# A kernel of recurrence, routing and six attention layers: the attention mask written by ACT instead of added by PE

## The chip, the cores and the metric

The kernel runs on one core of one Trainium2 chip. The core has a matrix engine (PE, whose weight loads are shown apart as PEld), three engines for elementwise work (DVE, ACT, POOL), a queue engine (SP) that issues transfers, and a PSUM memory of eight banks of 128 partitions by 512 float32 columns, into which PE writes. The metric is the device time of one execution in microseconds (us); lower is better.

## The reference

The reference has four parts, one after the other, on 16 sequences of 256 tokens with 128 channels: a gated recurrence, a routed feed-forward, a small linear attention, and a stack of six layers that takes most of the time. Each of the six layers is a local attention with 16 heads of 64 channels and a feed-forward. What the change touches is the attention:

```python
q, k = l2norm(q) * qs, l2norm(k) * ksc      # and a rotary turn
bq = q.reshape(b, h, nw, w, d)              # windows of w = 32 tokens
bk2, bv2 = look(bk), look(bv)               # own window and the one before: 64 keys
mask = (it < jb) | (it > jb + w) | (jb == -1)
sim = jnp.einsum('bhwie,bhwje->bhwij', bq, bk2) * QK_SCALE
sim = jnp.where(mask, -jnp.finfo(sim.dtype).max, sim)
attn = jax.nn.softmax(sim, -1)
out = jnp.einsum('bhwij,bhwje->bhwie', attn, bv2)
```

## The kernel before, in words

After a prologue for the first three parts, the six layers run as one software pipeline. A unit u is one layer with one of eight windows (NC = 8), 48 units in all (NU); a step n handles a quarter of a unit, four of the 16 sequences, so there are 192 steps (NG). Each engine has its own loop over n, written out by hand in its order, and semaphores join them. In its step n each engine works on several stages of different quarters at once; below, "step 0" to "step 3" are the steps with n % 4 (called q4) of 0 to 3, and four of them are a round.

On PE a step holds: the projections `proj(n, 0..5)` (line 550; parts 0 and 1 are q, 2 and 3 are k, 4 and 5 are v), transposed probabilities, products with the values, the output projection, and once a round the pieces of the feed-forward. For the quarter n - 2 it holds the key transposes `turn_k(n - 2, 0)` and `turn_k(n - 2, 1)` (line 570), the mask, and the scores `sim(n - 2)` (line 595): 128 small products into banks 4 and 5, one bank for each parity of the heads. Then come the query transposes of quarter n (line 560).

The scores of a bank are 128 rows (4 sequences by 32 queries) by 8 heads by 64 keys. `mask` (line 582) opens each bank: a product of a 32-row identity, idb, with a 512-column mask, mkb, both bf16, puts 0 or -1e36 into every column, with the flag that starts a sum. The score products then add to it. The two mask products use different rows of the array. idb and mkb are made once, at the start, by five ACT instructions (lines 1266 and 1270) from kc, a tile of constants that holds the mask for the 64 keys of one head, in three forms (first window, and two orders of the key buffer).

On ACT a step holds evacuations of banks: squares of q and k (`square`, 1358), values (`v_out`, 1366, tile vst), turned keys (`turned_k`, 1384, into kT, which the trace calls big), turned queries (`turned_q`, 1373), probabilities (1397), outputs (`out_turned`, 1405), the exponential (`exps`, 1390), and once a round gelu (1476), a shifted copy, and the copies of the norm (1448, 1449). DVE reads the scores (`largest`, 1049, and `lessened`, 1060, which raises v_sm and after which banks 4 and 5 are free) and turns q and k (1027, 1029); POOL scales and adds (1692, 1678, 1684, 1700).

Banks 2 and 3 are handed from use to use in program order: `claim` makes PE wait for whoever empties the bank. The second key transposes are in bank 2 and are emptied by `turned_k(n - 2, 1)`; the next user of bank 2 on PE is `variance` (651) in step 3, the third part of `gate` (674) in step 1, and the query transposes in the others. `sim` itself waits for both copies of the keys (a_tk). The last projection, part 5, uses bank 3. Lines in the profile are those of this kernel:

Of the kernel before, what the change touches and what calls it, by code (L numbers as in the profile page):

```python
# [8 lines left out]
BF16 = mybir.dt.bfloat16  # L9
# [147 lines left out]
def program(nc, x_d, kc_d, wa_d, wb_d, ba_d, tab_d, qs_d, wqkv_d, wo_d, w1_d, w2_d, vec_d, we_d, out_d, keep_d, xsort_d, ysort_d):  # L157
    with ExitStack() as ctx:
        def sb(name, shape, dt=F32):
# [21 lines left out]
        mkb = sb("mkb", [2 * W, 3, 512], BF16)  # L181
        idb = sb("idb", [2 * W, P], BF16)
# [34 lines left out]
            a_sq a_vst a_tq a_tk a_exp a_p2 a_oev a_xf a_hi a_halo a_mb a_x2s a_halo2 a_ln a_xn a_xh a_w1 a_gelu a_e a_w  # L217
# [160 lines left out]
        def _(eng):  # L378
# [195 lines left out]
            def mask(g):  # L574
                if not 0 <= g < NG:
                    return
                c = g // 4 % NC
                pe.wait_ge("a_mb", 5)
                for par in range(2):
                    pe.wait_ge("v_sm", 2 * (g - 1) + par + 1)  # L580
                    rows = slice(W * par, W * par + W)
                    eng.matmul(bank[4 + par][:, :], idb[rows, :], mkb[rows, 0 if c == 0 else 1 + c % 2, :], start=True, stop=False)  # L582

            def sim(g):
# [5 lines left out]
                pe.wait_ge("g_zero", 1)  # L590
                for r in range(8):
                    for par in range(2):
                        rows = slice(64 * par, 64 * par + 64)
                        for b in range(4):
                            m = eng.matmul(bank[4 + par][32 * b:32 * b + 32, 64 * r:64 * r + 64], qT[rows, g % 2, r, 32 * b:32 * b + 32],  # L595
                                           kT[rows, r, :, 4 * i + b, :], start=False, stop=(r == 7))
# [134 lines left out]
            for n in range(NG + 2):  # L731
# [28 lines left out]
                mask(n - 2)  # L760
# [479 lines left out]
        def _(eng):  # L1240
# [23 lines left out]
            msk = kc[0:2 * W, KC["mask"]].rearrange("p (v k) -> p v k", v=3)  # L1264
            for v in range(3):
                eng.activation(mkb[:, v, :].rearrange("p (r k) -> p r k", r=8), msk[:, v, :].unsqueeze(1).to_broadcast([2 * W, 8, 64]), ACT.Copy,
                               scale=1.0, bias=0.0).then_inc(s["a_mb"], 1)
            for n in range(2):
                rows = slice(W * n, W * n + W)
                eng.activation(idb[rows, :].rearrange("p (b t) -> p b t", b=4), kc[rows, rows].unsqueeze(1).to_broadcast([W, 4, W]), ACT.Copy,  # L1270
                               scale=1.0, bias=0.0).then_inc(s["a_mb"], 1)
# [565 lines left out]
```

## Time and profile before

| | us |
|---|---|
| median of 3 runs | 3678.64 |
| lowest and highest run | 3673.33, 3685.43 |
| span of the profiled execution (first to last instruction) | 3676.2 |
| PE busy in it | 3451.3 (94%) |
| DVE, ACT, POOL busy | 2806.8 (76%), 2365.2 (64%), 2815.1 (77%) |
| mean granted PE clock | 0.973 |

The profile gives no time of the profiled execution beyond its span; the span is 2.4 us below the median of the runs. Busy time is the union of an engine's instructions, and since matmuls are pipelined and their ends modelled, a PE that is busy all the time can still have gaps of issue inside. The timeline gives start and length of each instruction, with equal neighbours merged (x3); the chain of waits is followed back from the last instruction, at each step to what released it.

### The profile page before, as it was taken

The numbers are of one execution on the slowest core, as the hardware profiler recorded it, in microseconds if no ns is written. First come the engines' busy times: TensorE is split into PE (matmuls) and PEld (weight loads), VectorE is DVE, ScalarE is ACT, GpSimd is POOL, SyncE is SP. The second block draws the span as 40 slices with busy tenths as digits, with TensorE's granted clock in tenths as the row PEclk, the third lists the DMA queues.
The fourth block names the chain that finished last, engine by engine and source line by source line (L and its number), as shares of the span: only waits on it lengthen the run. The fifth ranks groups of instructions, "written<-read, shape, count | busy, mean of one in ns | idle before, by whom it ended". The sixth has DMA issues, their size and how long they took to land.

```text
span 3676.2 us, 148973 instructions
## 1 busy us (share of the span) xinstructions
PE 3451.3 (94%) x64612; PEld 2721.5 (74%) x64612; DVE 2806.8 (76%) x4876; ACT 2365.2 (64%) x4307; POOL 2815.1 (77%) x3470
## 2 busy tenths in 40 slices
PE   3799986999999999999999999999999999999997
PEld 2566544788877888777888778877788887788775
DVE  3477666888887888878888878887788888788863
ACT  3333223677766777777777677776677777777663
POOL 1355546998887888878888888888788888888772
PEclk9799997999999999999999999999999999999999
DMA  3333212111111111211111121112111111112110
GB/s 100 98 97 93 87 31 58 47 43 39 46 47 49 40 41 44 51 44 42 45 38 46 44 52 39 42 43 52 40 46 42 40 45 50 44 40 50 36 43 24
DMA packets 126733, 183.48 MB, mean 50 GB/s; under 512 B 29824, under 2 KB 61440, under 8 KB 126080
## 3 DMA queue, kind: packets, MB, share of 16 engines
q1 hardware_dynamic: 119232, 146.15, 15.8%
q0 software_dynamic: 6848, 27.80, 2.5%
q8 instruction: 511, 8.37, 1.0%
q14 instruction: 142, 1.16, 0.1%
HBM read 59.01 MB, written 14.16 MB: 20 GB/s over the span
## 4 chain that ended last, share of the span: by engine, by line
PE 85%; POOL 5%; DVE 3%; issue 3%; ACT 1%; DMA 1%; SPq 0%; ACTq 0%; POOLq 0%; DVEq 0%
PE bank L550 22%; PE bank L622 10%; PE bank L633 9%; PE bank L595 7%; PE bank L560 5%; PE bank L570 4%; PE bank L606 4%; PE bank L696 3%; PE bank L674 3%; PE bank L685 3%; PE bank L582 2%; PE bank L465 1%; PE bank L525 1%; PE bank L642 1%; PE bank L504 1%
## 5 line engine op out<-in xcount | busy, mean ns | idle before, releaser
L550 PE MATMUL bank<-wqkv,xs 128*128 128x512 f32 x3456 | 1061.5, 423 | 17.1 <-DVE m L1029 13.1
L1684 POOL TENSOR_TENSOR m<-m 128x512 f32<-128x512 f32 x576 | 728.7, 1285 | 45.2 <-DVE m L1029 42.6
L550 PEld LDWEIGHTS bank<-wqkv,xs 128*128 128x128 f32 x3456 | 582.8, 191 | 146.0 <-issue 56.9
L1029 DVE TENSOR_TENSOR m<-bank,tab 128x512 f32<-128x512 f32 x768 | 521.5, 679 | 0.7 <-POOL m L1684 0.3
L1358 ACT ACTIVATE sq<-bank 128x512 f32<-128x512 f32 x768 | 458.5, 597 | 98.1 <-PE bank L550 54.2
L1692 POOL TENSOR_TENSOR S<-S,nw 128x1024 f32<-128x1024 f32 x192 | 383.3, 1996 | 168.0 <-DVE S L1060 168.0
L1040 DVE TENSOR_REDUCE ss<-sq 128x8 f32<-128x512 f32 x768 | 504.9, 674 | 0.0
L1700 POOL TENSOR_TENSOR S<-S,rs 128x512 f32<-128x512 f32 x384 | 411.0, 1091 | 69.7 <-DVE rs L1074 67.9
L622 PEld LDWEIGHTS bank<-P,big 64*64 64x64 f32 x24576 | 379.6, 135 | 79.8 <-issue 72.3
L1027 DVE TENSOR_TENSOR m<-bank,tab 128x512 f32<-128x512 f32 x576 | 392.1, 681 | 57.4 <-ACT sq L1358 41.9
L633 PE MATMUL bank<-OT,wo 128*128 128x128 f32 x3072 | 389.9, 282 | 40.8 <-ACT P L1397 27.6
L622 PE MATMUL bank<-P,big 64*64 64x32 f32 x24576 | 401.9, 220 | 4.2 <-issue 3.2
L633 PEld LDWEIGHTS bank<-OT,wo 128*128 128x128 f32 x3072 | 371.8, 198 | 44.9 <-issue 44.6
L1366 ACT ACTIVATE vst<-bank 128x512 f32<-128x512 f32 x384 | 229.6, 598 | 272.6 <-PE bank L550 258.3
L1373 ACT ACTIVATE qT<-bank 128x512 f32<-128x512 f32 x384 | 210.1, 596 | 245.7 <-PE bank L560 245.4
L1684 POOL TENSOR_TENSOR mk<-mk,m 128x512 f32<-128x512 f32 x192 | 242.4, 1285 | 101.0 <-DVE m L1029 101.0
L595 PEld LDWEIGHTS bank<-big,qT 64*32 64x32 f32 x24576 | 265.0, 105 | 64.8 <-issue 62.8
L1049 DVE TENSOR_REDUCE mx<-bank 128x8 f32<-128x512 f32 x384 | 246.9, 684 | 84.5 <-PE bank L595 83.2
L595 PE MATMUL bank<-big,qT 64*32 64x64 f32 x24576 | 299.1, 226 | 6.5 <-issue 5.9
L1027 DVE TENSOR_TENSOR mk<-bank,tab 128x512 f32<-128x512 f32 x192 | 131.5, 685 | 197.7 <-ACT sq L1358 197.6
L1067 DVE TENSOR_REDUCE mx<-S 128x16 f32<-128x1024 f32 x192 | 232.4, 1210 | 16.9 <-ACT S L1390 14.2
L1060 DVE TENSOR_TENSOR S<-bank,mx 128x512 f32<-128x512 f32 x384 | 245.1, 679 | 0.0
(232 smaller groups left out, 6457.1 us busy)
## 6 DMA issues: line engine op xcount, KB each, us to landing
big<-vst SPq DMA_DIRECT2D x1536, 64.0 KB
stage<-in_wqkv SPq DMA_DIRECT2D x36, 256.0 KB, 3.0
tab<-in_tab SPq DMA_DIRECT2D x48, 128.0 KB, 2.2
xsort<-big SPq DMA_DIRECT2D x4, 960.0 KB, 8.6
big<-xsort SPq DMA_DIRECT2D x12, 256.0 KB, 4.5
ysort<-big SPq DMA_DIRECT2D x12, 256.0 KB, 3.6
wo<-in_wo SPq DMA_DIRECT2D x6, 512.0 KB, 3.7
big<-in_x SPq DMA_DIRECT2D x8, 256.0 KB, 3.4
```

Source lines behind the costliest of these rows:

```text
L550: m = eng.matmul(pb[:, :], xt[a], wqkv[:, z, 512 * part:512 * part + 512], start=(n == 0), stop=(n == 2))
L595: m = eng.matmul(bank[4 + par][32 * b:32 * b + 32, 64 * r:64 * r + 64], qT[rows, g % 2, r, 32 * b:32 * b + 32], kT[rows, r, :, 4 * i + b, ...
L622: m = eng.matmul(bank[6 + par][half:half + 64, 128 * k + 32 * b:128 * k + 32 * b + 32], V2[rows, 4 * i + b, 64 * r:64 * r + 64], P2[rows, ...
L633: m = eng.matmul(pb[:, 0:128], wo[:, r, :], OT[:, g % 2, r, :], start=(r == 0), stop=(r == 7))
L1027: eng.tensor_tensor(turned(g, part).rearrange("p (h d) -> p h d", d=DH), pv, ct.unsqueeze(1).to_broadcast([P, 8, DH]), ALU.mult)
L1029: eng.tensor_tensor(m2[:, s3, :].rearrange("p (h s d) -> p h s d", s=2, d=DH // 2), pw, sn.rearrange("p (s d) -> p s d", s=2).unsqueeze(1) ...
L1040: eng.tensor_reduce(ss[:, g // 2 % 2, a:a + 8], sq[:, part % 2, :].rearrange("p (h d) -> p h d", d=DH), axis=X_AX, op=ALU.add).then_inc(s[ ...
L1049: eng.tensor_reduce(mx[:, g % 2, 0, :].rearrange("p (r q) -> p q r", q=2)[:, par], bank[4 + par][:, :].rearrange("p (r k) -> p r k", r=8), ...
L1358: eng.activation(sq[:, part % 2, :], bank[part % 2][:, :], ACT.Square, scale=1.0, bias=0.0).then_inc(s["a_sq"], 1)
L1684: eng.tensor_tensor(turned(g, part), turned(g, part), m2[:, part % 2, :], ALU.add).then_inc(s["g_add"], 1)
L1692: eng.tensor_tensor(S16, S16, nw[:, g // 2 % 2, 1, 32 * (g % 2):32 * (g % 2) + 16].unsqueeze(2).to_broadcast([P, 16, 64]), ALU.mult).then_ ...
L1700: eng.tensor_tensor(S8, S8, rs[:, g % 2, 8 * h:8 * h + 8].unsqueeze(2).to_broadcast([P, 8, 64]), ALU.mult).then_inc(s["g_pn"], 1)
```

## The change

`mask` goes from PE. ACT gets `masked(g)`: for each of banks 4 and 5 one copy from kc, the 64 mask columns repeated for the eight heads, into the whole bank. It stands in ACT's step between the exponential (and what follows it in some steps) and `v_out(n, 0)`. It waits for v_sm as the product did, and for two prologue users of the banks. The scores wait for it by a new semaphore, a_mk; no product starts the sum in banks 4 and 5 any more, all of them add. The tiles mkb and idb and the five instructions that made them are gone.

```diff
--- before.py
+++ after.py
@@ -178,8 +178,6 @@
         zero = sb("zero", [P, NB])
         xs = sb("xs", [P, 2, 2, N], F32R)
         xf = sb("xf", [P, N])
-        mkb = sb("mkb", [2 * W, 3, 512], BF16)
-        idb = sb("idb", [2 * W, P], BF16)
         sq = sb("sq", [P, 2, 512])
         m1 = sb("m1", [P, 4, 512])
         m2 = sb("m2", [P, 2, 512])
@@ -214,7 +212,7 @@
             v_half v_rec v_u v_x1 v_x2 v_x3 v_rt v_xt v_rk v_he v_sh v_rb v_fs v_fn v_pr v_tq v_rc
             g_z g_n1 g_n2 g_n3
             p_proj p_tq p_tk p_sim p_pt p_av p_wo p_lnc p_lnv p_lnb p_fg p_fa p_fw p_ec p_ev p_eb
-            a_sq a_vst a_tq a_tk a_exp a_p2 a_oev a_xf a_hi a_halo a_mb a_x2s a_halo2 a_ln a_xn a_xh a_w1 a_gelu a_e a_w
+            a_sq a_vst a_tq a_tk a_exp a_p2 a_oev a_xf a_hi a_halo a_mk a_x2s a_halo2 a_ln a_xn a_xh a_w1 a_gelu a_e a_w
             v_w1 v_xl v_k v_ss v_sm v_max v_sum v_rec2 v_res v_lo v_ln v_xn v_h v_X v_back v_e v_out v_w
             g_zero g_add g_scl g_sub g_pn g_ch g_tab""".split()
         sems = {n: ctx.enter_context(nc.semaphore(n)) for n in names}
@@ -571,16 +569,6 @@
                 m.then_inc(s["p_tk"], 1)
                 vacant[RING["tk"][h]] = [("a_tk", 2 * g + h + 1)]
 
-            def mask(g):
-                if not 0 <= g < NG:
-                    return
-                c = g // 4 % NC
-                pe.wait_ge("a_mb", 5)
-                for par in range(2):
-                    pe.wait_ge("v_sm", 2 * (g - 1) + par + 1)
-                    rows = slice(W * par, W * par + W)
-                    eng.matmul(bank[4 + par][:, :], idb[rows, :], mkb[rows, 0 if c == 0 else 1 + c % 2, :], start=True, stop=False)
-
             def sim(g):
                 if not 0 <= g < NG:
                     return
@@ -588,12 +576,13 @@
                 pe.wait_ge("a_tq", 2 * g + 2)
                 pe.wait_ge("a_tk", 2 * g + 2)
                 pe.wait_ge("g_zero", 1)
+                pe.wait_ge("a_mk", 2 * g + 2)
                 for r in range(8):
                     for par in range(2):
                         rows = slice(64 * par, 64 * par + 64)
                         for b in range(4):
                             m = eng.matmul(bank[4 + par][32 * b:32 * b + 32, 64 * r:64 * r + 64], qT[rows, g % 2, r, 32 * b:32 * b + 32],
-                                           kT[rows, r, :, 4 * i + b, :], start=False, stop=(r == 7))
+                                           kT[rows, r, :, 4 * i + b, :], start=False, stop=(r == 7), skip_group_check=True)
                 m.then_inc(s["p_sim"], 1)
 
             def probs(g, h):
@@ -757,7 +746,6 @@
                 turn_k(n - 2, 0)
                 proj(n, 3)
                 turn_k(n - 2, 1)
-                mask(n - 2)
                 proj(n, 5)
                 if q4 == 3:
                     variance(u - 2)
@@ -1261,14 +1249,6 @@
                         eng.activation(h[:, :, t], step_in[:, n % 2, :], ACT.Tanh, scale=1.0, bias=0.0).then_inc(s["a_rec"], 1)
 
             ac.wait_ge("d_kc", 32)
-            msk = kc[0:2 * W, KC["mask"]].rearrange("p (v k) -> p v k", v=3)
-            for v in range(3):
-                eng.activation(mkb[:, v, :].rearrange("p (r k) -> p r k", r=8), msk[:, v, :].unsqueeze(1).to_broadcast([2 * W, 8, 64]), ACT.Copy,
-                               scale=1.0, bias=0.0).then_inc(s["a_mb"], 1)
-            for n in range(2):
-                rows = slice(W * n, W * n + W)
-                eng.activation(idb[rows, :].rearrange("p (b t) -> p b t", b=4), kc[rows, rows].unsqueeze(1).to_broadcast([W, 4, W]), ACT.Copy,
-                               scale=1.0, bias=0.0).then_inc(s["a_mb"], 1)
             for what, c, j in chunk_order("ACT"):
                 if what == "step":
                     steps(c, j, j + 1)
@@ -1383,6 +1363,19 @@
                 d = kT[:, 4 * h:4 * h + 4, c % 2, 4 * i:4 * i + 4, :].rearrange("p r b t -> p r (b t)")
                 eng.activation(d, bank[RING["tk"][h]][:, :].rearrange("p (r t) -> p r t", r=4), ACT.Copy, scale=1.0, bias=0.0).then_inc(s["a_tk"], 1)
 
+            def masked(g):
+
+                if not 0 <= g < NG:
+                    return
+                c = g // 4 % NC
+                v = KC["mask"].start + 64 * (0 if c == 0 else 1 + c % 2)
+                ac.wait_ge("v_rb", NC)
+                ac.wait_ge("v_tq", NC)
+                for par in range(2):
+                    ac.wait_ge("v_sm", 2 * (g - 1) + par + 1)
+                    eng.activation(bank[4 + par][:, :].rearrange("p (r k) -> p r k", r=8), kc[:, v:v + 64].unsqueeze(1).to_broadcast([P, 8, 64]),
+                                   ACT.Copy, scale=1.0, bias=0.0).then_inc(s["a_mk"], 1)
+
             def exps(g):
                 if not 0 <= g < NG:
                     return
@@ -1518,6 +1511,7 @@
                 if q4 == 3:
                     centred(u - 2)
                     end_centred(u - 5)
+                masked(n - 2)
                 v_out(n, 0)
                 square(n, 2)
                 turned_k(n - 2, 0)
```

Three places show how instructions move. First PE in a step 3, around the mask; L570 (L568 after) are the second key transposes, L550 (L548) the last projection, L651 (L640) the variance, L595 (L584) the scores. Before:

```order
L550 MATMUL bank<-wqkv,xs 128x512 [waits v_k]
L550 MATMUL bank<-wqkv,xs 128x512 x2
L570 MATMUL bank<-kc,mk 128x128 [waits a_vst,g_scl]
L570 MATMUL bank<-kc,mk 128x128 x3
L582 MATMUL bank<-mkb,idb 128x512 [waits v_sm] x2
L550 MATMUL bank<-wqkv,xs 128x512 [waits a_tk]
L550 MATMUL bank<-wqkv,xs 128x512 x2
L651 MATMUL bank<-kc,lnx 128x1 [waits a_tk]
L651 MATMUL bank<-kc,lnx 128x1 x3
L595 MATMUL bank<-big,qT 32x64 x64
```

After:

```order
L548 MATMUL bank<-wqkv,xs 128x512 [waits v_k]
L548 MATMUL bank<-wqkv,xs 128x512 x2
L568 MATMUL bank<-kc,mk 128x128 [waits a_vst,g_scl]
L568 MATMUL bank<-kc,mk 128x128 x3
L548 MATMUL bank<-wqkv,xs 128x512 [waits a_tk]
L548 MATMUL bank<-wqkv,xs 128x512 x2
L640 MATMUL bank<-kc,lnx 128x1 [waits a_tk]
L640 MATMUL bank<-kc,lnx 128x1 x3
L584 MATMUL bank<-big,qT 32x64 [waits a_mk]
L584 MATMUL bank<-big,qT 32x64 x63
```

The mask row is gone, so the projection follows the transposes, and the first score product waits for a_mk. Then ACT in a step 3, from the exponential to the first key copy. Before:

```order
L1390 ACTIVATE S<-S 128x1024 [waits g_sub]
L1465 ACTIVATE xnr<-xn 128x512 [waits p_fa,a_xn]
L1448 ACTIVATE lnx<-bank 128x512 [waits p_lnv,p_lnc]
L1449 ACTIVATE lnx<-bank 128x512
L1366 ACTIVATE vst<-bank 128x512 [waits d_v2,p_proj]
L1358 ACTIVATE sq<-bank 128x512 [waits v_ss,p_proj]
L1384 ACTIVATE big<-bank 128x4x128 [waits p_tk]
L1358 ACTIVATE sq<-bank 128x512 [waits v_ss,p_proj]
```

After:

```order
L1383 ACTIVATE S<-S 128x1024 [waits g_sub]
L1458 ACTIVATE xnr<-xn 128x512 [waits p_fa,a_xn]
L1441 ACTIVATE lnx<-bank 128x512 [waits p_lnv,p_lnc]
L1442 ACTIVATE lnx<-bank 128x512
L1376 ACTIVATE bank<-kc 128x512 [waits v_sm] x2
L1346 ACTIVATE vst<-bank 128x512 [waits d_v2,p_proj]
L1338 ACTIVATE sq<-bank 128x512 [waits v_ss,p_proj]
L1364 ACTIVATE big<-bank 128x4x128 [waits p_tk]
L1338 ACTIVATE sq<-bank 128x512 [waits v_ss,p_proj]
```

The two writes into banks stand ahead of the value evacuation (vst). Last, ACT at the start of the program, from its first table load. Before:

```order
L1266 ACT_TABLE_LOAD
L1266 ACTIVATE mkb<-kc 64x512 [waits d_kc]
L1266 ACTIVATE mkb<-kc 64x512 x2
L1270 ACTIVATE idb<-kc 32x128 x2
L1278 ACTIVATE big<-bank,ba 128x512 [waits p_px]
L1282 ACTIVATE big<-bank,hb 128x512 [waits v_half,p_px]
```

After:

```order
L1258 ACT_TABLE_LOAD [waits p_px]
L1258 ACTIVATE big<-bank,ba 128x512 [waits d_kc]
L1262 ACTIVATE big<-bank,hb 128x512 [waits v_half,p_px]
L1246 ACTIVATE big<-big 128x16 [waits a_px]
L1249 ACTIVATE big<-step_in 128x16 [waits v_rec] x22
```

The five instructions on mkb and idb are gone, and the table load comes after the wait for the first product. The orders of DVE, POOL and SP are the same in both.

## Rows read from the trace of the kernel before

**Rows 1.** The page, part 4: chain of waits, share of the span by engine.
```profile
PE 85%; POOL 5%; DVE 3%; issue 3%; ACT 1%; DMA 1%; SPq 0%; ACTq 0%; POOLq 0%; DVEq 0%
```

**Rows 2.** Windows, one round of four steps: length, busy us (instructions) per engine, clock, DMA.
```profile
1803.55:1864.33 60.78, 60.78 (x1303) 49.91 (x1302) 50.04 (x85) 45.05 (x79) 52.36 (x62) 1.00 0.18 43
```

**Rows 3.** Groups by line and shape, PE: busy us, mean ns | idle before.
```profile
L582 PE MATMUL bank<-mkb,idb 32*128 32x512 bf16 x384 | 74.7, 386 | 0.0
```

**Rows 4.** Timeline, step 3 at 1801 us: start us, length us, engine, line, operation.
```profile
1801.39 0.60 ACT L1366 ACTIVATE vst<-bank 128x512 f32<-128x512 f32 x1 [1.81 <-PE bank L550]
...
1801.88 0.60 PE L570 MATMUL bank<-kc,mk 128*128 128x128 f32 x4
...
1802.24 0.94 PE L550 MATMUL bank<-wqkv,xs 128*128 128x512 f32 x3
...
1803.02 0.60 PE L570 MATMUL bank<-kc,mk 128*128 128x128 f32 x4
...
1803.55 0.39 PE L582 MATMUL bank<-mkb,idb 32*128 32x512 bf16 x2
1803.71 0.59 ACT L1384 ACTIVATE big<-bank 128x512 f32<-128x512 f32 x1
...
1803.87 0.97 PE L550 MATMUL bank<-wqkv,xs 128*128 128x512 f32 x3
...
1804.44 1.09 PEld L651 LDWEIGHTS bank<-kc,lnx 128*128 128x128 f32 x8
...
1805.55 1.46 PEld L595 LDWEIGHTS bank<-big,qT 64*32 64x32 f32 x128
```

**Rows 5.** Timeline, the program's last step with score products.
```profile
3590.30 1.08 ACT L1384 ACTIVATE big<-bank 128x512 f32<-128x512 f32 x2 [0.81 <-PE bank L570]
...
3591.44 0.46 PEld L674 LDWEIGHTS bank<-xnr,w1r 128*85 128x85 f32 x3 [0.71 <-ACT big L1384]
...
3592.30 0.93 PE L595 MATMUL bank<-big,qT 64*32 64x64 f32 x71
```

**Rows 6.** Chain of waits, the same place.
```profile
3590.80 0.60 ACT big L1384
...
3591.44 0.93 PE bank L674 x3
```

**Rows 7.** Timeline, step 0 at 1813 us.
```profile
1813.35 1.06 ACT L1390 ACTIVATE S<-S 128x1024 f32<-128x1024 f32 x1
...
1815.39 0.60 ACT L1366 ACTIVATE vst<-bank 128x512 f32<-128x512 f32 x1 [0.98 <-PE bank L550]
...
1816.09 0.60 ACT L1358 ACTIVATE sq<-bank 128x512 f32<-128x512 f32 x1
...
1817.72 0.59 ACT L1384 ACTIVATE big<-bank 128x512 f32<-128x512 f32 x1
...
1818.77 1.49 PE L595 MATMUL bank<-big,qT 64*32 64x64 f32 x128
```

**Rows 8.** Timeline, step 1 at 1829 us.
```profile
1829.68 0.60 ACT L1366 ACTIVATE vst<-bank 128x512 f32<-128x512 f32 x1 [1.00 <-PE bank L550]
...
1832.01 0.59 ACT L1384 ACTIVATE big<-bank 128x512 f32<-128x512 f32 x1
...
1832.97 0.85 PE L674 MATMUL bank<-xnr,w1r 128*85 128x512 f32 x3
...
1833.75 1.58 PE L595 MATMUL bank<-big,qT 64*32 64x64 f32 x128
```

**Rows 9.** Tile mkb: duration ns min/median/max, first and last start us.
```profile
L1266 ACT ACTIVATE mkb<-kc x3: 617/619/635, 6.8 to 7.9; 64x512 bf16<-64x512 f32 x3
```

**Rows 10.** Timeline, step 2 at 1844 us.
```profile
1844.73 0.60 ACT L1366 ACTIVATE vst<-bank 128x512 f32<-128x512 f32 x1 [1.53 <-PE bank L550]
```

**Rows 11.** Timeline, ACT at the program's start.
```profile
9.06 0.69 ACT L1278 ACTIVATE big<-bank,ba 128x512 f32<-128x512 f32 x1
```

**Rows 12.** Chain of waits at a layer's end.
```profile
2050.93 6.75 DMA stage<-in_wqkv x2
```

## The prediction

> **What bounds the kernel now.** I read the chain of waits first: its head puts 85% of the span on PE [rows 1]. Then the busy time of one round of four steps in the steady part: in 60.78 us PE is busy for 60.78, DVE 50, ACT 45, POOL 52, at a granted clock of 1.00, which is the 2.4 GHz level [rows 2]. So every stretch that PE is spared shortens the run, until another engine's result comes too late. The groups by line give the mask products 74.7 us of busy time, 386 ns each where one stood alone, and 192 pairs [rows 3]. That is time of the pair's own; what PE really gives up is read in the timeline, from the start of the work before it to the start of the work after.
>
> **What PE is spared.** In the step at 1801 us the key transposes start at 1803.02 and the next projection at 1803.87, 0.85 us later, with the mask pair between. The earlier key transposes of the same step, with no mask behind them, start at 1801.88 and their projection at 1802.24: 0.36 us [rows 4]. The difference, **0.49 us a step**, is the price of a mask pair on PE with the idle array before and behind it; in 192 steps 94 us.
>
> The Trainium skill (TensorE: Matmul & The Clock Gate, "Back-to-back issue gap") has a matmul of 512 columns cost about 216 ns at the full clock; by that rule the pair, which runs side by side, would be worth 0.22 us a step and 42 us in all. The trace disagrees: the gaps around the pair are its own, since the same handover without it takes 0.36 us.
>
> **What takes the place of the mask.** PE needs ACT's copy of the second key transposes (L1384) soon after: the score products read kT, and where a gate or a variance product comes before them it claims bank 2, which that copy frees. The copy hangs on the square of the projection before it and on the transposes, both older than the mask, so it does not move when the mask goes. How fast PE follows is seen in the two steps at the end that have no last projection. There PE waits for the copy already: the pair of copies runs from 3590.30 for 1.08 us, to 3591.38, and the weights of the gate product start at 3591.44; weights are not loaded ahead of the wait [rows 5]. The chain has the second copy alone, 3590.80 for 0.60, and PE at 3591.44 [rows 6]: 0.04 us after its end, which I take. Four kinds of step:
> - step 0 (every fourth): the copy starts at 1817.72, takes 0.59, and lets PE go at 1818.35. The scores start at 1818.77 now, and would at 1818.28 without the mask [rows 7]. PE waits 0.07, gain 0.42 us. Step 2 has the same distances: gain 0.42.
> - step 1: the copy starts at 1832.01 and releases PE at 1832.64. The gate product runs at 1832.97 now and would at 1832.48 [rows 8]: 0.16 late. Its weights could not be loaded ahead either: from a gated start to the scores it takes 0.86 us [rows 5] against 0.78 [rows 8]. Loss 0.24, gain 0.25.
> - step 3: eight small products (L651) come first, paced by their weights, whose loads run from 1804.44 for 1.09 us straight into the scores at 1805.55. Without the mask they would start at 1803.95; the copy (from 1803.71) releases them at 1804.34 [rows 4]. Loss 0.39, gain **0.10**.
>
> Sum of a round: 0.42 + 0.25 + 0.42 + 0.10 = 1.19 us, and 48 rounds make 57 us. So about two fifths of the 94 us turn into a wait for ACT.
>
> **What ACT takes on.** Two writes of 128x512 from kc, spread over eight heads, into a bank. No row shows ACT writing a bank. The nearest is its copy of this very mask into mkb: 619 ns, and three of them started between 6.8 and 7.9 us, so one every 0.54 us [rows 9]. Copies out of a bank follow each other at 1.08 - 0.59 = 0.49 [rows 5]. So a pair costs 0.98 to 1.08 us; I take 1.08 by the row with the same source. With 4 pairs a round ACT goes from 45 to 49 us of 60: not the bound.
>
> The pair stands before v_out(n, 0) (the value evacuation, vst), and that is where ACT waits for PE: 1.81 us in step 3 [rows 4], 0.98 in step 0 [rows 7], 1.00 in step 1 [rows 8], 1.53 in step 2 [rows 10], and about 0.1 more each since one ACT instruction starts before the last has ended. So the pair hides: in steps 0 and 1 with nothing to spare, in 2 and 3 easily. Behind v_out the next square has 0.2 us of slack (1815.39 + 0.49 against 1816.09 [rows 7]), and an ACT that is late by more delays square, copy and PE one for one. In step 1 the exponential waits for POOL, which the shorter steps don't move: some 0.15 us, inside that slack. I charge nothing. If the cover were gone, a pair would cost up to 1.08 us a step.
>
> The wait on v_sm in front of the writes is for the subtraction of the step before, which the exponential just ahead of them on ACT has already needed. Behind the writes on ACT's queue stand v_out, the squares that DVE's rotation waits for, and the key copies; none becomes late while the cover holds. DVE, POOL and SP keep their order; DVE and POOL have 8 to 11 us of air in a round [rows 2], and no PE row of the steps read names either in a wait.
>
> **Small terms.** At the start five ACT instructions go. The first projection's bias runs at 9.06 us, while its constants were there at 6.8 [rows 9, 11]: 2 us gained, as the recurrence behind it is a chain. At each of five layer ends the chain runs through a weight transfer of 6.75 us [rows 12] and not through PE; I take two steps a boundary at 0.3 us as lost, 3 us. The last two steps wait for the copy today: 1 us lost.
>
> **The sum**: 57 + 2 - 3 - 1 = 55 us. The profiled execution spans 3676.2 us, so 3621 after; the median of the runs is 2.4 us above that span, and on its scale **3624 us**, 1.5% less. A measurement of this kernel tells about 0.3%, 11 us, from nothing.
>
> **Rivals.**
> - *No wait for the copy* (A). If ACT's copy lands earlier or weights are loaded ahead of the wait, all of 94 us comes: 94 + 2 - 3 - 1 = 92, **3587 us**. Against: rows 5 show weights loaded only after the copy. Chance 0.08.
> - *The gap stays* (B). The mask could go and the array still idle around the handover, so that only the pair's own streaming is saved. Bounds: half of 0.49, 0.24 us. Then steps 0 to 2 gain 0.24 each and step 3 its 0.10: 0.82 a round, 39 us, with the small terms 37: **3642 us**. By the 0.22 us of the Trainium skill (TensorE: Matmul & The Clock Gate, "Back-to-back issue gap") it would be 3644. For it: row groups change at the scores anyway. Against: the 0.36 us without a mask [rows 4]. Chance 0.16.
> - *ACT's cover runs out* (C). If a write into a bank costs 0.85 us, a pair takes 1.7 and steps 0 and 1, which can hold about 1.3, lose 0.4 each; 0.8 of the 1.19 is gone, 38 us: 55 - 38 = 17, **3662 us**. For it: the cover in steps 0 and 1 is as long as the pair. Against: broadcast source and length are those of a row of 0.54. Chance 0.07.
> - *Slower* (D). The same mechanism past its break-even. With c the cost of a pair, steps 0 and 1 lose c - 1.3 each and steps 2 and 3 begin to lose at about 1.8 and 2.1 (their idle time and the slack behind). Against the gain of 1.19 it decides at c of about 1.9 us, a little under 1 us a write; the exponential's 1.06 us for 1024 columns [rows 7] is the nearest row of that length. At c = 2.4, 1.2 us a write: 1.1 + 1.1 + 0.6 + 0.3 = 3.1 lost a round, net 1.9 x 48 = 91 slower, **3770 us**. It needs twice the time that any 512-column ACT instruction takes here. Chance 0.03.
> - *The change does not do what it says* (E). If another engine's pace showed as PE's, nothing moves: 3677 us. The full PE of rows 2 speaks against. 0.04. A second form of it leaves the time alone: the sums need PE to add to what ACT wrote. The Trainium skill (PSUM — Partial Sum Buffer, "The four PSUM rules") says a product without the start flag adds only where an earlier product has marked the elements, and overwrites otherwise; no run here shows it yet.
>
> **The numbers.** The forecast case, 3605 to 3640 for 0.25 to 0.15 us of uncertainty in the step 1 and 3 losses and in the handover, has 0.62. The 8-in-10 range goes on to B and a part of C, **3597 to 3650**; A, D, E and most of C, 0.2 together, stay out. Faster by over 0.3%: forecast, A, B and most of C, 0.92. Within: E and a little of C, 0.05. Slower: D, 0.03.
>
> **What the profile after would show.** The mask line gone from PE; the projection 0.36 us behind the second key transposes in each step; PE's idle time before L595, the gate line and L651 naming ACT's key copy, in about 0.07, 0.16 and 0.4 us; the round at 59.6 us. ACT's two writes start about 0.54 apart, and its wait before vst shrinks to nothing in steps 0 and 1 and to 0.5 to 0.8 in the others. Wrong would be: PE waiting for squares or projections' banks (C or D), a handover still at 0.6 us (B), step 3 gaining as much as step 0 (A).

## The result and the profile after

The changed kernel takes **3656.2 us**, median of four runs (3652.2 to 3660.7), against 3676.0 before in the same runs: a ratio of 0.994, 95% interval [0.992, 0.996]. It is faster, but by 20 us where 55 were forecast, and 3656 lies outside the range of 3597 to 3650. The profiled execution spans 3650.4 us, 25.8 less than that of before. The ratios below leave out one execution of e3, which took 5353 us at a mean granted clock of 0.577.

The page after the change: the span, the busy time of each engine, and the chain of waits by engine ([rows 1] before).

```profile
span 3650.4 us, 148686 instructions
PE 3384.4 (93%) x64228; PEld 2688.0 (74%) x64228; DVE 2806.7 (77%) x4876; ACT 2529.7 (69%) x4686; POOL 2814.3 (77%) x3470
...
PE 76%; ACT 6%; POOL 6%; issue 5%; DVE 4%; DMA 1%; SPq 0%; POOLq 0%; ACTq 0%; DVEq 0%
```

PE's share of the chain falls from 85% to 76%, ACT appears with 6%, and "issue", time in which PE waited for nothing that the profile shows, grows from 3% to 5%. The last figure is the one that matters.

**What came as forecast.** The timeline of a step 3 and of the step 0 behind it ([rows 4] and [rows 7] before; start, length, then [idle before <- released by]):

```profile
1788.55 1.14 ACT L1376 ACTIVATE bank<-kc 128x512 f32<-128x512 f32 x2
...
1790.48 0.60 ACT L1346 ACTIVATE vst<-bank 128x512 f32<-128x512 f32 x1 [0.79 <-PE bank L548]
...
1792.11 0.60 PE L568 MATMUL bank<-kc,mk 128*128 128x128 f32 x4
...
1792.47 0.94 PE L548 MATMUL bank<-wqkv,xs 128*128 128x512 f32 x3
1792.81 0.59 ACT L1364 ACTIVATE big<-bank 128x512 f32<-128x512 f32 x1
1793.45 0.97 PEld L640 LDWEIGHTS bank<-kc,lnx 128*128 128x128 f32 x8 [0.47 <-ACT big L1364]
...
1794.43 1.46 PEld L584 LDWEIGHTS bank<-big,qT 64*32 64x32 f32 x128
...
1804.45 1.12 ACT L1376 ACTIVATE bank<-kc 128x512 f32<-128x512 f32 x2
...
1805.71 0.60 ACT L1346 ACTIVATE vst<-bank 128x512 f32<-128x512 f32 x1
...
1807.35 0.60 PE L568 MATMUL bank<-kc,m 128*128 128x128 f32 x4
...
1807.70 0.94 PE L548 MATMUL bank<-wqkv,xs 128*128 128x512 f32 x3
...
1808.68 1.32 PEld L584 LDWEIGHTS bank<-big,qT 64*32 64x32 f32 x128 [0.47 <-ACT big L1364]
```

The projection follows the second key transposes after 0.35 to 0.36 us, as without a mask. The variance weights and the scores wait for ACT's key copy, and are let go 0.05 us behind its end (1792.81 + 0.59, and 1793.45). ACT's pair of writes takes 1.12 to 1.14 us (forecast 1.08) and lies where ACT had waited for PE: in step 0 vst starts with no wait left, in step 3 with 0.79 us. A round that nothing disturbs, as windows of before (first) and after (second):

```profile
2687.53:2748.06 60.53, 60.53 (x1306) 49.67 (x1304) 50.04 (x84) 45.07 (x79) 52.27 (x62) 1.00 0.20 48
```

```profile
2846.68:2906.06 59.38, 59.20 (x1297) 49.09 (x1296) 50.03 (x86) 48.42 (x87) 52.38 (x61) 1.00 0.17 41
2723.26:2785.73 62.47, 59.57 (x1298) 49.13 (x1296) 51.84 (x87) 49.15 (x88) 52.96 (x61) 1.00 0.16 39
```

The gain of such a round is 1.15 us, where 1.19 were forecast: 55 us in 48 rounds. But the third window, also of the changed kernel, has the same PE work and takes 3.1 us more.

**What did not.** Two lines of the waits of before, PE waiting:

```profile
PE bank L595 <- issue: 5.9, 11, 0.9
PE bank L560 <- issue: 3.7, 7, 1.0
```

and the same places after (scores and query transposes; us in total, times, longest):

```profile
PE bank L584 <- issue: 33.4, 28, 1.7
PE bank L558 <- issue: 7.3, 8, 1.5
```

That is 31 us of new stalls, and the gain of the undisturbed rounds, 55 us, less 31 is 24, near the 25.8 by which the spans differ. That it fits so closely is in part luck, since the start of the six layers alone moves by several microseconds from run to run (below). One of them, in the step 0 at 2796 us of the changed kernel: PE breaks off in the middle of the score products, after 88 of 128.

```profile
2796.20 1.10 PE L584 MATMUL bank<-big,qT 64*32 64x64 f32 x88
2798.48 0.50 PEld L584 LDWEIGHTS bank<-big,qT 64*32 64x32 f32 x40 [1.34 <-issue]
2798.48 0.66 PE L584 MATMUL bank<-big,qT 64*32 64x64 f32 x40 [1.18 <-issue]
```

**Where it breaks off.** The page's part on DMA queues has a queue of its own for instructions; its line in the changed kernel is "q8 instruction: 508, 8.32, 0.9%": 508 blocks of 16 KB. PE has 130186 records in that trace, so 256 instructions to a block. Counting PE's records from the start, 43 of the 55 breaks of over 0.75 us between 650 and 3500 us come at the same place of a block (record 193 of 256, to within a few), which is therefore its edge. Before the change 10 of 25 do. In front of each such break a block is being fetched, and the fetch starts late. Edges do not fall on the scores more often than before: between 650 and 3500 us each of the two kernels has 85 blocks that begin between 90 instructions ahead of the first score and 25 behind it, so that the next edge falls late in the scores or just behind them. The step above, and a step of before, which has an edge in its scores too and no break:

| step at | last wait instruction of PE ahead of the scores | fetch starts | first score | break at the edge |
|---|---|---|---|---|
| 2820 us, before | 2817.72 | 2818.87 | 2820.47 | none |
| 2796 us, after | 2795.06 | 2796.07 | 2796.20 | 1.2 us |

The Trainium skill (Runtime: NRT & Kernel Launch, "Instruction fetch mechanics") says that the sequencer fetches its instructions in blocks of 16 KiB, 256 instructions, the next page while the current one runs, and that crossing is "mostly hidden". Sizes and numbers agree with the trace; "hidden" doesn't here: the scores of a step have 256 instructions (128 products and their weight loads) in about 1.5 us.

### The profile page after: what moved, and what is told of

It is laid out like the page before. It is cut to its first block, busy times and chain, and to the rows that moved or that the text cites. A ratio compares the mean times of both kernels' runs of the same rounds, so it can differ in the third digit from the quotient of the medians.

```text
span 3650.4 us, 148686 instructions
## 1 busy us (share of the span) xinstructions
PE 3384.4 (93%) x64228; PEld 2688.0 (74%) x64228; DVE 2806.7 (77%) x4876; ACT 2529.7 (69%) x4686; POOL 2814.3 (77%) x3470
## 3 DMA queue, kind: packets, MB, share of 16 engines
q8 instruction: 508, 8.32, 0.9%
q14 instruction: 145, 1.19, 0.1%
## 4 chain that ended last, share of the span: by engine, by line
PE 76%; ACT 6%; POOL 6%; issue 5%; DVE 4%; DMA 1%; SPq 0%; POOLq 0%; ACTq 0%; DVEq 0%
PE bank L548 18%; PE bank L611 10%; PE bank L622 9%; PE bank L584 7%; PE bank L558 5%; PE bank L595 4%; PE bank L685 4%; PE bank L663 3%; PE bank L674 3%; PE bank L568 2%; ACT big L1364 2%; ACT sq L1338 2%; PE bank L523 1%; PE bank L463 1%; PE bank L631 1%
## 5 line engine op out<-in xcount | busy, mean ns | idle before, releaser
L548 PE MATMUL bank<-wqkv,xs 128*128 128x512 f32 x3456 | 1058.2, 422 | 19.6 <-DVE m L1017 13.6
L548 PEld LDWEIGHTS bank<-wqkv,xs 128*128 128x128 f32 x3456 | 584.0, 191 | 104.6 <-issue 13.2
L584 PEld LDWEIGHTS bank<-big,qT 64*32 64x32 f32 x24576 | 268.5, 105 | 107.5 <-issue 56.4
L584 PE MATMUL bank<-big,qT 64*32 64x64 f32 x24576 | 306.3, 227 | 38.3 <-issue 33.4
L1346 ACT ACTIVATE vst<-bank 128x512 f32<-128x512 f32 x384 | 232.9, 606 | 74.2 <-PE bank L548 73.5
L1383 ACT ACTIVATE S<-S 128x1024 f32<-128x1024 f32 x192 | 203.3, 1059 | 75.3 <-POOL S L1686 72.5
```

The source lines that it names most:

```text
L548: m = eng.matmul(pb[:, :], xt[a], wqkv[:, z, 512 * part:512 * part + 512], start=(n == 0), stop=(n == 2))
```

## The experiments

The first theory was that PE's new wait for the key copy, right ahead of the scores, holds its sequencer back (theory 1). Its rivals: PE is simply denser without the mask (2), ACT's writes are the cause (3). The four runs after the result:

**e1.** On PE `turn_k(n - 2, 1)` ahead of `proj(n, 3)`, on ACT `turned_k(n - 2, 1)` ahead of `square(n, 3)`:

```diff
                 turn_k(n - 2, 0)
-                proj(n, 3)
                 turn_k(n - 2, 1)
+                proj(n, 3)
```

> The changed kernel, with the second key transposes (PE) and their copy (ACT) moved ahead of projection 3 and its square. Theory 1 (PE stands at the wait for ACT's second key copy, and because it is held there it asks for its next block of instructions too late, which gives the stalls inside the scores): the copy is over 1 us early, the 48.5 us that PE's weight loads of the scores waited for it go, and of the 33 us of issue stalls in the scores most go too (under 10 us left); 3580 to 3600 us, 0.975 to 0.980 of before. Theory 2 (the stalls come from where the blocks' edges fall in a denser stream, wait or no wait): the waits go, the stalls stay at about 30 us; 3605 to 3620 us. Theory 3 (ACT's writes or ACT's load hold the program): no gain over the changed kernel, 3645 to 3660 us.

Measured: ratio 1.002 [1.001, 1.003], 3702 us against 3693 of before on that chip. The waits of this run:

```profile
PE bank L584 <- issue: 34.9, 34, 1.9
...
PE bank L568 <- ACT vst L1346: 19.4, 35, 1.1
PE bank L568 <- DVE xn L1095: 18.9, 43, 0.7
```

The wait for the copy is gone from the weights of the scores (1.0 us is left of 48.5), and the stalls are all there: theory 1 falls. The time is above what any of the three theories gave. The move costs two new waits, since the second key transposes now need bank 2 sooner than ACT and DVE leave it (steps 0 and 2).

**e2.** `sim` gets a half h: r runs over four of its eight values and waits for the key copy of that half alone.

```diff
                 turn_k(n - 2, 1)
+                sim(n - 2, 0)
                 proj(n, 5)
...
-                sim(n - 2)
+                sim(n - 2, 1)
```

> The changed kernel, with the scores issued in two halves: heads of copy 0 right behind the second key transposes, projection 5 and what follows it, then heads of copy 1. Theory 1: no wait for the second copy is left, and the dense run is cut in two with a projection of 1.27 us between, so almost no stall in the scores; 3575 to 3600 us. The first half may wait for the first copy for a few tenths of a microsecond. Theory 2: the stalls shrink here too, the waits go: 3580 to 3605 us; this run tells the two apart only with the run before. Theory 3: 3645 to 3660 us.

Measured: 0.995 [0.994, 0.997]. Stalls before the scores 16.8 us, the copy waits mostly gone (1.4 us on PE and 9.3 on its weight loads are left), and as much lost to the split: the score products are busy for 347.2 us where they took 306.3. The time is in the range of theory 3, but the stalls halved with ACT's writes still there. Groups by line of this kernel and of the changed one:

```profile
L584 PE MATMUL bank<-big,qT 64*32 64x64 f32 x24576 | 347.2, 224 | 18.3 <-issue 16.8 <-ACT big L1366 1.4
```

```profile
L584 PE MATMUL bank<-big,qT 64*32 64x64 f32 x24576 | 306.3, 227 | 38.3 <-issue 33.4 <-ACT big L1364 0.7
```

**e3.** In the kernel before:

```diff
                 proj(n, 3)
+                mask(n - 2)
                 turn_k(n - 2, 1)
-                mask(n - 2)
```

> The kernel before, mask still two products on PE, but issued ahead of the second key transposes, so that nothing but projection 5 lies between these and the scores. Theory 1: PE must wait for the second copy as in the changed kernel (about 37 us beyond before) and the stalls in the scores come up from 6 to about 30 us: 3730 to 3755 us, 1.015 to 1.021 of before. Theory 2 (stalls need the mask gone from PE): 3705 to 3720 us, stalls in the scores still about 6 us. Theory 3 (the stalls come from ACT's writes): as theory 2.

Measured: 1.005 [1.003, 1.007].

```profile
PE bank L595 <- issue: 4.5, 9, 0.8
```

```profile
PEld bank L595 <- ACT big L1384: 44.1, 101, 0.9
```

The waits for the copy are nearly those of the changed kernel (44.1 against 48.5 us, 101 times each), the stalls those of before. So the wait for the copy is not what brings the stalls, and theory 1 falls a second time. The run is also faster than either range (1.008 to 1.021): the mask pair costs less PE time there (transposes 0.31 us behind its start, 1806.16 and 1806.47). Whether that is the whole difference, no run shows.

**e4.** In the kernel before, ACT's two writes as well (`masked` as in the change, counting on a_mb); the mask products overwrite them.

```diff
-                    pe.wait_ge("v_sm", 2 * (g - 1) + par + 1)
+                    pe.wait_ge("a_mb", 5 + 2 * g + par + 1)
```

> The kernel before, and ACT writes the mask into the score banks as well (in the changed kernel's place), the products on PE write over it and wait for ACT's writes in place of DVE's last read. Theories 1 and 2: the writes lie in ACT's waiting time and PE's order is as before: 3670 to 3690 us, stalls in the scores about 6 us. Theory 3: the writes alone cost 25 us or more, 3700 us and over.

Measured: 1.001 [1.000, 1.002]; stalls before the scores 9.2 us. ACT's writes alone do next to nothing: against theory 3.

**A fourth theory.** In e1 the fetches start as late as in the changed kernel, in e3 as early as before. What e1 and the changed kernel share is not a wait that lasts, but a wait instruction. This is how the first score product stands in the program's order, with the semaphores that it needs, before and after, in a step 0 or 2:

```
L595 MATMUL bank<-big,qT 32x64 [waits a_tk]
L584 MATMUL bank<-big,qT 32x64 [waits a_mk,a_tk]
```

One semaphore rides on the product's first instruction. With two there is a wait instruction of its own (a record of 0.05 us at L49): PE has 1626 of them before and 1726 after; two a round make 96 of the 100. In steps 1 and 3 the gate or variance product takes a_tk, the scores need a_mk alone, and the stalls are few there. Take the blocks that begin between 90 instructions ahead of the first score and 25 behind it, and the break at their end, 256 instructions on: on average it is 1.37 and 0.94 us in steps 0 and 2, 0.2 to 0.3 in steps 1 and 3. Theory 4: PE's sequencer does not pass such an instruction before its time, and so asks for the next block after it.

**e5.** In `sim` of the changed kernel:

```diff
                 pe.wait_ge("g_zero", 1)
-                pe.wait_ge("a_mk", 2 * g + 2)
```

ACT writes the mask before it copies the keys, so a_tk covers it.

> The changed kernel without PE's wait for ACT's mask writes ahead of the scores (the wait for ACT's second key copy, which ACT does after them, covers it). Theory 4, new: a first instruction that needs two semaphores gets a wait instruction of its own ahead of it; PE's sequencer stands there, and asks for its next block of instructions only after it. In steps 0 and 2 of a round the scores need a_mk and a_tk, in steps 1 and 3 a_mk alone, and before they needed a_tk alone. So the stalls of over 0.4 us at the blocks' edges in the scores fall from 43 to about 20, as before the change, and the fetches that start 0.1 us behind the first score start about 1.5 us ahead of it again: 30 to 40 us faster than the changed kernel, 0.983 to 0.987 of before. Theory 2 (the products of the mask gave the time that the fetch needs): no difference from the changed kernel, 0.992 to 0.996.

Measured: **0.989** [0.986, 0.991], 3641.9 us against 3680.0.

```profile
PE bank L583 <- issue: 16.3, 22, 1.4
```

Half of the stalls before the scores go (33.4 to 16.3 us); the longer breaks (over 0.4 us) fall from 43 to 35, not to 20, and the time is not as low as theory 4 had it (0.983 to 0.987). Theory 4 holds for a part.

**e6.** The reverse, in `sim` of the kernel before; the semaphore has long been there:

```diff
                 pe.wait_ge("a_tk", 2 * g + 2)
+                eng.wait_ge(s["a_mb"], 5)
```

> The kernel before, with one wait more ahead of the scores, on a semaphore that has long been there (a_mb, 5), so that it never has to wait: only the wait instruction of its own is added. Theory 4: the stalls of over 0.4 us in the scores rise from 19 to about 40, in steps 0 and 2, and it gets 20 to 40 us slower, 1.005 to 1.011 of before. Theory 2: no change, 0.999 to 1.002.

Measured: 1.004 [1.002, 1.005].

```profile
PE bank L596 <- issue: 27.9, 30, 1.3
```

From 5.9 to 27.9 us, breaks from 19 to 39, by an instruction that never waits, with mask and ACT unchanged. This is the plainest of the runs. The time, 14 us more, is below the 20 to 40 us that were expected.

In step 0, for blocks that begin 15 to 85 instructions ahead of the first score: the median start of the next block's fetch relative to the first score, and the mean break at the edge to that next block (10 or 11 cases each, from the trace's instruction queue):

| kernel | fetch starts | break |
|---|---|---|
| before | -1.53 us | 0.21 us |
| e6, before with the extra wait | -0.42 | 1.32 |
| changed | +0.13 | 1.35 |
| e5, changed without it | -0.97 | 0.49 |

**e7.** e5, and e1's move in steps 1 and 3 alone, on PE and likewise on ACT:

```diff
                 turn_k(n - 2, 0)
+                if q4 % 2:
+                    turn_k(n - 2, 1)
                 proj(n, 3)
-                turn_k(n - 2, 1)
+                if q4 % 2 == 0:
+                    turn_k(n - 2, 1)
```

> e5, and in steps 1 and 3 of each round alone the second key transposes and their copy ahead of projection 3 and its square (in steps 0 and 2 the run with all four showed them waiting for bank 2). From the undisturbed steps of that run (14.6 and 16.7 us against 14.8 and 17.0 of the changed kernel) 0.5 us a round more, 24 us: 0.977 to 0.981 of before if theory 4 holds, 0.986 to 0.990 if it doesn't.

Measured: 0.990 [0.988, 0.993], no better than e5, and the value that had been put down for theory 4 not holding. But the gain was eaten elsewhere: steps 1 and 3 do come down to 14.6 and 16.7 us, while the undisturbed step 0 goes from 12.6 to 13.1. PE now waits 28 times for ACT's key copy ahead of a projection, 7.0 us in all; what else lengthens step 0 is open. So this run says nothing on theory 4.

**e8.** The changed kernel without `masked`, so that the mask is left out of the computation and every score product starts its own sum. In `sim`, beside two waits on long fulfilled semaphores of the prologue:

```diff
-                pe.wait_ge("a_mk", 2 * g + 2)
+                for par in range(2):
+                    pe.wait_ge("v_sm", 2 * (g - 1) + par + 1)
```

> The changed kernel with the mask left out of the computation: ACT writes nothing into the score banks, and PE waits ahead of the scores for DVE's last read of them in place of ACT's writes (two semaphores again). Theories 2 and 4: as the changed kernel, 0.992 to 0.996 of before, stalls in the scores about 40. Theory 3 (ACT's writes or its load cost time): 0.985 or less.

Measured: 1.000 [0.999, 1.002], a miss of every theory's number.

```profile
PE bank L587 <- issue: 55.0, 40, 1.8
```

The scores now need v_sm ahead of them in place of a_mk, and there are more wait instructions (1817 of them), in steps 1 and 3 too. In steps 1 the mean break is 1.2 us now, but in steps 3 it stays at 0.2: most fetches there start about 1 us ahead of the wait instruction. Leaving the writes out saved nothing visible; the stalls are 22 us more than in the changed kernel. Steps 1 go with theory 4, steps 3 show that it is not complete, and the run was meant for theory 3 and does not settle it.

**e9 to e12** ran on one chip. e9 is the changed kernel again.

> The changed kernel once more, unaltered, to have it on the same chip as the three others: 0.992 to 0.996 of before, about 33 us of issue stalls before the matmuls of the scores.

Measured: 0.996 [0.995, 0.998], stalls before the scores 36.3 us.

**e10.** e5 without the two writes, their waits kept on ACT; again the mask is left out of the computation, and every score product starts its own sum. In `masked`:

```diff
                     ac.wait_ge("v_sm", 2 * (g - 1) + par + 1)
-                    eng.activation(bank[4 + par][:, :].rearrange("p (r k) -> p r k", r=8), kc[:, v:v + 64].unsqueeze(1).to_broadcast([P, 8, 64]),
-                                   ACT.Copy, scale=1.0, bias=0.0).then_inc(s["a_mk"], 1)
```

> e5 (no wait for the mask on PE) without the mask: ACT keeps the waits and leaves its two writes out, so that PE's instructions and waits are those of e5 exactly. Theories 2 and 4 (ACT's writes lie in its waiting time): as e5, within 0.2%, 0.986 to 0.990 of before. Theory 3 (the writes delay ACT's key copy or the V writes): 10 us or more under e5, 0.985 or less.

Measured: 0.990 [0.989, 0.992], as e5 within the intervals, stalls 16.8 us. ACT's writes cost nothing that could be told: theory 3 is out.

**e11.** e5, with the scores split as in e2 in 31 steps chosen from e5's trace:

```diff
+                if n in SPLIT:
+                    sim(n - 2, 0)
                 proj(n, 5)
...
-                sim(n - 2)
+                sim(n - 2, 1 if n in SPLIT else None)
```

> e5, with the scores split around projection 5 only in the 31 steps in which the trace of e5 shows a block's edge where the next block is late in the scores (steps 0 and 2 of a round, edge from 90 instructions before to 26 behind the first score). If the stall is a fixed time from the request of the block to its use, the 1.27 us of the projection between the halves hide most of it: of e5's stalls of 24 us before the scores and query transposes under 10 are left, at 0.25 us for each split (8 us): 8 to 15 us under e5, 0.984 to 0.987 of before. If the stall lies in the dense run itself, no gain, 0.988 to 0.991.

Measured: 0.990 [0.988, 0.991], stalls 11.7 before the scores and 5.7 before the query transposes, against 16.3 and 7.5; under 10 in all had been expected. The 6 us that this saves are about what 31 splits at 0.2 us cost, and the time does not move.

**e12.** The same on e7.

> e7 (key transposes first in steps 1 and 3) with the same 31 steps split: e11 and what e7 gained in steps 1 and 3 (profile: 6 us of the middle part): 0.981 to 0.986 of before.

Measured: 0.988 [0.986, 0.990], short of the 0.981 to 0.986 expected. It is the lowest ratio, but its interval overlaps that of e5, which differs from the changed kernel by one deleted line.

**What was open then**: e5 keeps 14 us more of stalls (16.3 + 7.5) than the kernel before (5.9 + 3.7), and theory 4 had not told the place of the wait instruction from its being there.

**e13, e14.** e5 with two needless products ahead of projection 5, or (e14, with `part == 4`) of projection 4. In `proj`:

```diff
+                for _ in range(2 if part == 5 else 0):
+                    eng.matmul(pb[:, :], xt[0], wqkv[:, 0, 512 * part:512 * part + 512], start=True, stop=True)
```

> e5 with two needless products ahead of projection 5 (its first product, whose result the projection then writes over): 4 instructions and about 0.46 us a step of PE's time, 88 us in all, in the place where the mask's products had stood. Theory 2 as what is left beside theory 4 (the time of the products just ahead of the scores hides part of a block's fetch, and all of the wait for the second copy): stalls before the scores fall from 16 to about 6 us as in the kernel before, waits for the copy go; 30 to 45 us over e5, 0.997 to 1.001 of before. If the place means nothing: 80 to 90 us over e5, 1.010 to 1.014.

> The same two products ahead of projection 4, before the key transposes, so that their time is not between these and the scores. Theory 2: stalls before the scores stay at 15 to 20 us and the waits for the copy stay; 75 to 90 us over e5, 1.009 to 1.014 of before. If the place means nothing: as the run before this.

Measured: near 0.999 [0.998, 1.000], far 1.012 [1.010, 1.014]. The waits for the copy, near and then far:

```profile
PEld bank L585 <- ACT big L1365: 35.6, 96, 1.0
...
PEld bank L664 <- ACT big L1365: 1.1, 1, 1.1
```

```profile
PEld bank L585 <- ACT big L1365: 48.5, 101, 0.9
PEld bank L664 <- ACT big L1365: 22.0, 45, 1.1
PEld bank L641 <- ACT big L1365: 21.9, 46, 0.5
```

The same PE work costs some 48 us less (1.3% of 3690) where the copy is waited for. That is the wait that the prediction put at 37 us (94 less 57), from another side and somewhat larger; 4 us of it lie ahead of the six layers in the two profiles (first projection at 590.5 and 594.9 us). But the stalls before the scores are 9.2 us near and 10.4 far, where 6 against 15 to 20 had been expected: that the products stand right ahead of the scores does not decide them.

**e15.** The a_mk wait ahead of `turn_k(n - 2, 1)` instead of the scores:

```diff
                 proj(n, 3)
+                if 0 <= n - 2 < NG:
+                    eng.wait_ge(s["a_mk"], 2 * (n - 2) + 2)
                 turn_k(n - 2, 1)
```

> The changed kernel with PE's wait for ACT's mask writes taken ahead of the second key transposes, in all steps: as many waits, but none of its own ahead of the scores. Theory 4 by place (the last wait instruction ahead of a dense run sets when the next block is asked for): as e5, 0.987 to 0.991, stalls before the scores about 16 us. If the number of wait instructions counts and not the place: 0.994 or more, stalls 30 us and over.

Measured: 0.990 [0.988, 0.992].

```profile
PE bank L583 <- issue: 14.4, 20, 1.5
PE bank L558 <- issue: 6.8, 8, 1.1
```

The time is that of e5. But this run does not part place from number, as its expectation says it would. The second key transposes had a wait instruction already, and one such instruction can hold two semaphores: 223 do in this run, 34 in the changed kernel. So PE has 1628 wait instructions here, two more than e5 and not the 1726 of the changed kernel. What it shows is that the same wait, joined to one that stands there anyway, costs nothing.

**What the traces say of the place.** Wait instructions stand in every step of the kernel before as well; what differs is how far ahead of the first score the last one runs. In steps 0, medians of all such steps between 650 and 3500 us, with the mean break for blocks that begin 15 to 85 instructions ahead of the first score (12 to 15 cases each), and the stalls before the scores of the whole run:

| kernel | last wait instruction ahead of the first score | break | stalls |
|---|---|---|---|
| e3, mask ahead | 2.75 us | 0.0 us | 4.5 us |
| before | 2.74 | 0.2 | 5.9 |
| e4, mask twice | 2.56 | 0.3 | 9.2 |
| e13, filler near | 2.52 | 0.2 | 9.2 |
| e14, filler far | 2.35 | 0.2 | 10.4 |
| e10, no writes | 2.20 | 0.4 | 16.8 |
| e5, no extra wait | 2.14 | 0.5 | 16.3 |
| e15, wait moved | 2.12 | 0.4 | 14.4 |
| e7, keys first in two | 1.96 | 0.6 | 16.7 |
| e6, extra wait before | 1.53 | 1.3 | 27.9 |
| changed | 1.13 | 1.4 | 33.4 |
| e1, keys first | 1.07 | 1.6 | 34.9 |

The nearer the last wait instruction is to the scores, the longer the break, whatever was changed; only neighbours in the table that are within 0.1 us of each other's breaks swap places. (e9 repeats the changed kernel's values, e8 has 1.13 and 1.4 us and further stalls in steps 1, and e2, e11 and e12 split the scores.) That bears out the place, and it goes for what e5 keeps as well: without the mask pair, 0.49 us of PE's time is missing between the last wait instruction and the scores. The stalls of e13 and e14 fit in too, though why the fillers of e14, which stand far ahead, lengthen the distance is open. Only e6 against before moves this distance and little else; the rest is read from the traces and not tested by a run of its own.

## Why the prediction was wrong

- *Spared, 0.49 us a step*: right. The handover takes 0.35 to 0.36 us, as without a mask; rival B (0.6) falls.
- *Waits for the key copy*: right in kind and nearly in size. The gains by kind of step are 0.3, 0.27, 0.41 and 0.19 us for steps 0 to 3, against 0.42, 0.25, 0.42 and 0.10: medians of the steady rounds for steps 1 to 3, and for steps 0 the undisturbed ones, 12.9 and 12.6 us. The median of all steps 0, measured from query transposes to query transposes, grows from 12.9 to 13.7 us with the stalls in it. The variance product in step 3 starts as forecast, but its weight loads then take 0.97 us and not the 1.09 of [rows 4], so that step loses less. Rival A falls: waits of the weight loads name the copy, 48.5 us for the scores, 22.0 for the gate and 21.9 for the variance.
- *ACT's cover*: right. No row of the waits names the writes, and e10 prices them at nothing that could be told. ACT's wait ahead of vst fell from 258.3 to 73.5 us in the run. C and D fall.
- *PSUM*: PE adds to what ACT wrote, with no start flag, and the score products are busy for 306.3 us against 299.1 before; the second form of E did not occur.
- *Small terms*: the first projection starts at 580.0 us instead of 584.4, but other runs have it anywhere from 575 to 597, so the 2 us at the start can't be told.
- **The failed step** is "PE waits for the copy" as the whole price of the new dependence, and with it "The sum: 57 + 2 - 3 - 1". I asked how long PE would wait for ACT's copy, and the new wait on a_mk ahead of the scores, which is fulfilled early, has no term in the sum. The wait that never waits was the dear one: with a_tk it makes two semaphores, in steps 0 and 2 a wait instruction of its own, and some 17 us of stalls (33.4 to 16.3), 20 us in time (e5 against the changed kernel: 0.989 and 0.994; e10 against e9 on one chip: 0.990 and 0.996). Some 14 us more of stalls stay with e5. They came with the mask's going: in steps 0 the last wait instruction lies 2.14 us ahead of the scores there and 2.74 before, which the table behind e15 sets beside the breaks, but no run tests this part alone. How the sequencer comes to ask for its block then stays open.

The result lies between rivals B and C in time and has the mechanism of neither. The sign of what happened could have been read before: 11 breaks of "issue" in the scores, 0.9 us the longest, at a step whose products and weight loads are 256 instructions in about 1.5 us. The prediction has no term for them.

## What to carry to other kernels

When a change gives an engine another semaphore to wait for, look at where the wait lands, not only at when it is fulfilled: ahead of a dense run of small instructions a second semaphore can cost more than the wait that it stands for. Drop a wait that an in-order engine's later signal already covers (e5), or join it to one that stands a few long instructions earlier anyway (e15). And when a change takes work from the bounding engine, add up the "issue" time in its densest stretch as a term of its own.

## What the runs showed of the hardware

- PE's instructions come in blocks of 256 (16 KB, about 1.05 us of transfer). In steps 0 a fetch starts some 1.1 to 1.25 us after the last wait instruction ahead of the scores (medians, in each of the kernels that do not split the scores), and where it starts late PE resumes about 2.5 us after the fetch's start (median of the changed kernel; up to 2.7 in others). What this time consists of, no run tells apart, and in steps 3 of e8 the fetch starts ahead of the wait instruction.
- A wait instruction on a semaphore fulfilled long ago cost 14 us, right ahead of the dense run in 96 steps (e6). One wait instruction holds one or two semaphores, and a wait that joined one already there, 2.1 us ahead of the scores, cost nothing (e15).
- Splitting a run of 128 small products in two costs some 0.2 us (e2: 41 us of busy time in 192 steps).
